# Layer 2 attention: scores of a pair of heads in one block, value products in one block, output projection in one burst

## The chip, the core and the metric

The kernel runs on one core of one Trainium2 chip. The metric is the device time of one execution in microseconds (us). A core has five engines with their own in-order instruction streams, which meet only through semaphores: TensorE (PE; its weight loads are listed as PEld), VectorE (DVE), ScalarE (ACT), GpSimd (POOL) and SyncE (SP). Matmuls write to PSUM, which has eight banks of 128 partitions x 512 float32.

## The reference

Four layers run one after the other over 16 sequences of 256 tokens and 128 channels (4096 tokens). Each layer computes `x = x + attention(layernorm(x)) * silu(ffn(layernorm(x)))`. The change touches the attention of layer 2 alone:

```python
q = z @ wq @ fcq_w + fcq_b          # 16 heads of 64 channels; k and v likewise
scores = jnp.einsum('bihd,bjhd->bhij', q, k) / scale
attn = jax.nn.softmax(scores, axis=-1)
out = jnp.einsum('bhij,bjhd->bihd', attn, v)
return out.reshape(b, n, 16 * 64) @ fco_w + fco_b
```

The feed-forward part of layer 2 is a mixture of eight experts (two chosen for each token). The kernel runs it in the same loop as the attention.

## The kernel before

**Tiling.** Tokens are taken in eight groups of 512 (two sequences each, called batch elements 0 and 1 of the group). Sixteen heads make eight pairs. A pair of heads of one group is a "pair"; there are 64. A pair and one batch element is a "unit" `n`; there are 128 (`ALL`). A unit has two halves, one for each head: half `h = 2n + half`. All matmuls are float32, and the trace shows each as two instructions.

**The loop.** `Layer2.tensor`, `.scalar` and `.vector` walk over the same slots, one unit for each slot, and each engine does, in this written order, what is due at a lag behind the slot (`due(slot, lag)`):

- PE: scores of unit `slot` (`tensor_score`, both halves, 64 rows of the array for each); in some slots a value projection ("v", called V below); transposes of half 0 of unit `slot - 2` (`tensor_turn`, T0 below); the product with the values of unit `slot - 3` (`tensor_times_v`, 64 columns of the array for each head); the projection of the next pair's q or k ("qk"); transposes of half 1 of unit `slot - 2` (T1); every second slot the output projection of a finished pair (`tensor_fold`); then expert work (`tensor_experts`: in even slots down and place, in odd slots up, from slot 32 to 104).
- DVE: reciprocal of the sums and normalisation of half 0 of unit `slot - 1`; the two row maxima of unit `slot` (`vector_max`); the V eviction; the copy of T0's bank to `pt` (`vector_turned`, unit `slot - 2`); normalisation of half 1 of unit `slot - 1`; the q or k eviction; routing or notes (`vector_notes`, even slots).
- ACT: expert evictions of the slot before; four exponentials of unit `slot` (`scalar_exp`); the copy of T1's bank (`scalar_turned`); every second slot the copy of the value products (`scalar_outputs`).
- POOL normalises the first 12 units, then issues indirect DMAs.

V occurs in slots 4 to 7 and 12 to 15 of every 16, that is in half of the pairs. The 64 pairs thus split in pairs with V and pairs without. I call slots 32 to 104, with expert work in each, the heavy slots, and the slots without expert matmuls the light ones. Slots 108 to 111 and 118 to 121 hold the joins of expert results, which keep PE busy far longer than a light slot.

**Waits and banks.** There is one bank for the transposes (`b_turn`): T1 of a unit waits for DVE's copy of T0, and T0 of the next unit waits for ACT's copy of T1 (`wait_turned_scores`). Scores have three banks; V and q/k projections share `b_misc`, and each waits until the last result there has been evicted. The scores of a pair wait for its q and k evictions (`l2_qk`). The output projection has a bank of its own (`b_fo`) in which it accumulates over eight slots' worth of pairs.

Of the kernel before, what the change touches and what calls it, by code (L numbers as in the profile page):

```python
# [12 lines left out]
P = 128  # L13
BATCH, SEQ = 16, 256
TOKENS = BATCH * SEQ
GW = 512
# [1828 lines left out]
L2_UNITS = BPG * L2_PAIRS  # L1845


class Layer2:
# [5 lines left out]
    def __init__(self, k, n, nth):  # L1854
# [12 lines left out]
        self.p, self.pt, self.o, self.mixed = work.ring(6), work.ring(4), region.ring(2), work.ring(GROUPS)  # L1867
# [3 lines left out]
        self.b_score, self.b_moe, self.b_turn, self.b_o, self.b_misc, self.b_fo = b[0:3], b[3], b[4], b[5], b[6], b[7]  # L1871
# [74 lines left out]
    def shared_bank(self, slot, kind):  # L1946

        return (self.b_misc, self.b_fo)[self.shared_count(slot, kind) % 2 if slot < 0 else 0]
# [21 lines left out]
    def vector_shared(self, v, on, slot, kinds):  # L1970
        s = self.k.sem
        for kind, g, i in self.shared(slot):
            if kind not in kinds:
                continue
            if kind == "v":
                c, t = divmod(i, TPG)
                on.wait_ge(s["l2_misc"], self.shared_count(slot, "v"))
                on.wait_ge(s["l2_pv"], L2_UNITS * (g - 1) + L2_UNITS // 2 * (c + 1))
# [15 lines left out]
    def tensor_score(self, pe, on, n, half):  # L1994
# [4 lines left out]
        on.wait_ge(s["l2_exp"], 2 * (h - 2))  # L1999
        q, kk = self.q[pair % 2][r, t], self.kk[pair % 2][r, t]  # L2000
        for i in range(2):
            last = mm(pe, self.b_score[h % 3][:, i * SEQ:(i + 1) * SEQ], q[:, i * P:(i + 1) * P], kk)
        last.then_inc(s["l2_score"], 1)

    def vector_max(self, v, on, n, half):
# [3 lines left out]
        v.tensor_reduce(self.mx[h % 8][:, 0:2], self.b_score[h % 3][:, :].rearrange("p (i j) -> p i j", j=SEQ), AX.X,  # L2009
# [6 lines left out]
    def scalar_exp(self, a, on, n, half):  # L2016
# [4 lines left out]
        for i in range(2):  # L2021
            c = slice(i * SEQ, (i + 1) * SEQ)
            a.activation(self.p[h % 6][:, c], self.b_score[h % 3][:, c], ACT.Exp, bias=self.mx[h % 8][:, i:i + 1],  # L2023
# [33 lines left out]
    def vector_turned(self, v, on, n):  # L2057
        s, h = self.k.sem, 2 * n
        on.wait_ge(s["l2_pt_mm"], h + 1)
        on.wait_ge(s["l2_pv"], n - 1)  # L2060
        v.tensor_copy(self.pt[h % 4], self.b_turn[:, :]).then_inc(s["l2_pt"], 1)  # L2061

    def scalar_turned(self, a, on, n):
        s, h = self.k.sem, 2 * n + 1
        on.wait_ge(s["l2_pt_mm"], h + 1)
        on.wait_ge(s["l2_pv"], n - 1)
        a.activation(self.pt[h % 4], self.b_turn[:, :], ACT.Copy).then_inc(s["l2_pt_act"], 1)

    def tensor_times_v(self, pe, on, n):
        s = self.k.sem  # L2070
        g, m, b = self.unit(n)
        self.wait_turned_scores(on, 2 * n)
        self.wait_turned_scores(on, 2 * n + 1)
        on.wait_ge(s["l2_v"], 8 * g + 4 * (m // 4) + 4)
        on.wait_ge(s["l2_o"], n // BPG)
        for jc in range(2):
            for half in range(2):
                h, r = 2 * m + half, half * L2_DH
                c = slice((h % 8) * L2_DH, (h % 8 + 1) * L2_DH)
                last = mm(pe, self.b_o[r:r + L2_DH, b * SEQ:(b + 1) * SEQ], self.v[2 * b + jc][h // 8][:, c],  # L2080
                          self.pt[(2 * n + half) % 4][:, jc * SEQ:(jc + 1) * SEQ], first=jc == 0, last=jc == 1)
        last.then_inc(s["l2_pv"], 1)

    def scalar_outputs(self, a, on, pair):
        s = self.k.sem
        on.wait_ge(s["l2_pv"], 2 * pair + 2)
        on.wait_ge(s["l2_fold"], pair - 1)
        a.activation(self.o[pair % 2], self.b_o[:, :], ACT.Copy).then_inc(s["l2_o"], 1)

    def tensor_fold(self, pe, on, pair):  # L2090
        s = self.k.sem
        g, m = divmod(pair, L2_PAIRS)
        on.wait_ge(s["l2_o"], pair + 1)
        if m == 0:
            on.wait_ge(s["l2_mixed"], g)
        mm(pe, self.b_fo[:, :], self.Fo[:, m, :], self.o[pair % 2], first=m == 0, last=m == L2_PAIRS - 1).then_inc(s["l2_fold"], 1)

    def scalar_mixed(self, a, on, g):
        s = self.k.sem
        on.wait_ge(s["l2_fold"], L2_PAIRS * (g + 1))  # L2100
        a.activation(self.mixed[g], self.b_fo[:, :], ACT.Identity, bias=self.o_b).then_inc(s["l2_mixed"], 1)
# [90 lines left out]
    def pair_end(self, slot, lag):  # L2192
        n = slot - lag
        return n // BPG if 0 <= n < self.ALL and n % BPG == BPG - 1 else None

    def tensor(self, pe, on):
# [5 lines left out]
        for slot in range(self.FIRST, self.LAST):  # L2202
# [10 lines left out]
            if (n := self.due(slot, 3)) is not None:  # L2213
                self.tensor_times_v(pe, on, n)
# [3 lines left out]
            if (n := self.pair_end(slot, 4)) is not None:  # L2218
                self.tensor_fold(pe, on, n)
            self.tensor_experts(pe, on, slot)  # L2220

    def scalar(self, a, on):
# [4 lines left out]
        for slot in range(self.FIRST, self.LAST):  # L2227
# [9 lines left out]
            if (n := self.pair_end(slot, 3)) is not None:  # L2237
                self.scalar_outputs(a, on, n)
            if (n := self.pair_end(slot, 4)) is not None and n % L2_PAIRS == L2_PAIRS - 1:
                self.scalar_mixed(a, on, n // L2_PAIRS)  # L2240
# [1635 lines left out]
```

## Time and profile before

| | us |
|---|---|
| median of 3 runs (range) | 2921.56 (2917.99 to 2922.57) |
| span of the profiled execution | 2983.9 |
| layer 2's loop in that span, from its first scores to its last output | 1357 to 2170 |
| slots 32 to 104 of it | 1566 to 2001 |

The span runs from the first to the last instruction of the profiled execution; no time outside of the span is recorded for it. The span is 62.3 us over the median of the timed runs. Over the whole span PE is busy 90%, DVE 65%, ACT 44% and POOL 42%.

### The profile page before, as it was taken

To read this page: it belongs to the slowest core of one execution; us is meant where nothing else is said; L and a number is where in the kernel's file an instruction comes from. 1 tells how busy PE (TensorE), PEld (TensorE's weight loads), DVE (VectorE), ACT (ScalarE), POOL (GpSimd) and SP (SyncE) were. 2 spreads that over 40 slices of the span, in tenths; PEclk is the share of its full clock that TensorE was granted. 3 is DMA by queue.
4 is the path that set the end of the run, shared out by engine and by line. 5 is a ranking of instruction groups with operands and counts; after the bars stand their busy time and mean duration, and the time that the engine had idled before them with its cause. 6 is when DMAs were issued, how large, how long until landed. Compare 5 with 4: busy or idle time off the path is not lost.

```text
span 2983.9 us, 40531 instructions
## 1 busy us (share of the span) xinstructions
PE 2684.1 (90%) x14378; PEld 1731.9 (58%) x14378; DVE 1941.2 (65%) x3806; ACT 1320.6 (44%) x3421; POOL 1239.8 (42%) x1116
## 2 busy tenths in 40 slices
PE   6899699999999999978879999999987988988888
PEld 3465245555555555544446666665546877766766
DVE  5778576877877777647657777776665272646633
ACT  4454424334344344344446666664542223355442
POOL 2553067677677677734542333320001340333331
PEclk8899799999999999989999999999977776889898
DMA  4453200000000000028012222211002211212113
GB/s 164 137 181 113 98 1 1 1 1 1 1 1 1 1 1 1 1 92 214 31 49 56 65 69 67 69 52 41 8 32 94 68 57 43 60 29 65 33 47 92
DMA packets 172520, 159.55 MB, mean 53 GB/s; under 512 B 98736, under 2 KB 149168, under 8 KB 171504
## 3 DMA queue, kind: packets, MB, share of 16 engines
q1 hardware_dynamic: 149536, 90.92, 10.9%
q0 software_dynamic: 22784, 66.05, 7.2%
q8 instruction: 115, 1.88, 0.3%
q14 instruction: 85, 0.70, 0.1%
HBM read 127.16 MB, written 59.51 MB: 63 GB/s over the span
## 4 chain that ended last, share of the span: by engine, by line
PE 42%; DVE 7%; ACT 3%; issue 2%; another core or an unknown queue 1%; DMA 0%; POOL 0%; SPq 0%; POOLq 0%; DVEq 0%; ACTq 0%
PE bank L65 37%; PE bank L2053 4%; DVE work L2009 1%; DVE work L3289 1%; ACT L3231 1%; DVE work L3071 0%; ACT weights_odd L2937 0%; DVE work L3337 0%; DVE work L1986 0%; DVE weights_odd L3339 0%; DVE weights_odd L3337 0%; DVE work L3488 0%; PE bank L2884 0%; DVE weights_even L3289 0%
## 5 line engine op out<-in xcount | busy, mean ns | idle before, releaser
L1492 POOL TENSOR_TENSOR work<-work 128x512 f32<-128x512 f32 x384 | 494.8, 1289 | 305.6 <-DVE work L1484 285.4
L65 PE MATMUL bank<-work 64*128 64x256 f32 (+5 forms) x4384 | 588.2, 351 | 23.4 <-DVE work L3488 7.2
L65 PE MATMUL bank<-weights_odd,normed_channels 128*128 128x512 f32 (+3 forms) x1152 | 520.4, 561 | 52.7 <-DVE work L1484 52.0
L65 PEld LDWEIGHTS bank<-work 64*128 64x128 f32 (+4 forms) x4384 | 412.4, 171 | 225.1 <-issue 144.7
L1484 DVE TENSOR_TENSOR work<-bank,work 128x512 f32<-128x512 f32 x360 | 244.4, 685 | 104.2 <-PE bank L65 100.3
L2023 ACT ACTIVATE work<-bank,work 128x256 f32<-128x256 f32 x512 | 236.0, 472 | 156.3 <-DVE work L2009 145.9
L65 PEld LDWEIGHTS bank<-weights_odd,normed_channels 128*128 128x128 f32 x1152 | 187.4, 198 | 183.2 <-DVE work L1484 94.2
L2009 DVE TENSOR_REDUCE work<-bank 128x2 f32<-128x512 f32 x256 | 165.3, 685 | 172.3 <-PE bank L65 151.5
L595 POOL DMA_INDIRECT weights_even<-in_L_Wx,expert_slots x112 | 111.6, 996 | 355.6 <-PE bank L668 270.9
L1559 ACT ACTIVATE work<-bank,work 128x256 f32<-128x256 f32 x256 | 119.0, 470 | 290.1 <-DVE work L1546 289.9
L65 PE MATMUL bank<-work,weights_odd 128*128 128x512 f32 (+3 forms) x520 | 209.3, 518 | 34.3 <-ACT work L3253 9.0
L65 PE MATMUL bank<-weights_even,work 128*128 128x128 f32 (+4 forms) x1568 | 219.4, 300 | 14.8 <-ACT work L3037 7.0
L65 PEld LDWEIGHTS bank<-weights_even,work 128*128 128x128 f32 (+2 forms) x1568 | 202.3, 206 | 30.9 <-issue 14.4
L2053 PEld LDWEIGHTS bank<-constants,work 128*128 128x128 f32 x1024 | 122.9, 142 | 149.0 <-issue 131.2
L65 PE MATMUL bank<-work,weights_even 32*128 32x128 f32 (+4 forms) x800 | 170.7, 403 | 39.9 <-DVE work L1037 11.4
L2053 PE MATMUL bank<-constants,work 128*128 128x128 f32 x1024 | 160.6, 280 | 21.9 <-DVE work L2061 10.3
L65 PE MATMUL bank<-weights_even 128*128 128x128 f32 (+3 forms) x940 | 175.5, 342 | 5.3 <-ACT work L3267 2.1
L2919 POOL TENSOR_TENSOR weights_odd<-weights_odd 128x512 f32<-128x512 f32 x40 | 52.4, 1309 | 291.1 <-ACT weights_odd L2914 291.1
L65 PE MATMUL bank<-weights_odd 128*128 128x128 f32 (+3 forms) x664 | 146.9, 373 | 8.2 <-ACT weights_odd L2891 5.9
L585 POOL DMA_INDIRECT noted_rows<-work,expert_slots x96 | 99.1, 1032 | 114.9 <-DVE work L575 88.4
L2041 DVE TENSOR_SCALAR work<-work 128x256 f32<-128x256 f32 x464 | 143.8, 352 | 4.1
L1621 POOL TENSOR_TENSOR work<-work 128x512 f32<-128x512 f32 x120 | 135.7, 1141 | 18.8 <-DVE work L1611 12.9
(343 smaller groups left out, 4633.6 us busy)
## 6 DMA issues: line engine op xcount, KB each, us to landing
filter_matrices<-in_L_filters SPq DMA_DIRECT2D x24, 512.0 KB, 8.1
work<-filter_matrices SPq DMA_DIRECT2D x16, 768.0 KB
weights_even<-noted_rows SPq DMA_DIRECT2D x56, 132.0 KB
noted_rows<-in_empty SPq DMA_DIRECT2D x11, 660.0 KB, 10.3
noted_rows_in<-in_empty SPq DMA_DIRECT2D x8, 660.0 KB, 10.2
weights_odd<-noted_rows_in SPq DMA_DIRECT2D x40, 132.0 KB
work<-token_rows SPq DMA_DIRECT2D x16, 256.0 KB, 3.0
token_rows_out<-in_zeros SPq DMA_DIRECT2D x6, 640.0 KB, 20.1
```

The source lines that it names most:

```text
L65: return pe.matmul(out, lhsT, rhs, start=first, stop=last, skip_group_check=True)
L585: gp.indirect_dma_start(self.x_rows[:, :], to, self.stage[g % len(self.stage)][:, i, :], None).then_inc(k.sem[f"rows_moved{self.moved_by(g ...
L595: gp.indirect_dma_start(self.W_of(m, i), None, self.weights, of).then_inc(self.k.sem[f"weights_moved{m % self.ring}"], 16)
L1484: v.tensor_tensor(heads(dst), heads(self.b_prod[p % 2][:, :]), self.per_head(self.score[g % 3], tile, kind == 0, e), ALU.mult).then_inc(s[ ...
L1492: gp.tensor_tensor(self.sum_of(p), self.sum_of(p), self.product_of(p), ALU.add).then_inc(s["l1_add"], 1)
L1559: a.activation(self.p[n % 2][:, c], self.b_score[n % 2][:, c], ACT.Exp, bias=self.mx[n % 4][:, i:i + 1], accum_out=self.sums(bt)[:, h, i:i ...
L1621: gp.tensor_tensor(self.kept[n % 2].rearrange("p (d h) -> p h d", h=L1_H), heads(self.o[i]), self.per_head(self.mask[g % 3], tile, 1, e), ...
L2009: v.tensor_reduce(self.mx[h % 8][:, 0:2], self.b_score[h % 3][:, :].rearrange("p (i j) -> p i j", j=SEQ), AX.X, ALU.max, negate=True).then ...
L2023: a.activation(self.p[h % 6][:, c], self.b_score[h % 3][:, c], ACT.Exp, bias=self.mx[h % 8][:, i:i + 1], accum_out=self.sums(n, half, i)). ...
L2041: eng.tensor_scalar(p[:, c], p[:, c], self.sums(n, half, i), None, ALU.mult).then_inc(s["l2_p"], 1)
L2053: last = pe.transpose(self.b_turn[:, jc * SEQ + i * P:jc * SEQ + (i + 1) * P], self.p[h % 6][:, i * SEQ + jc * P:i * SEQ + (jc + 1) * P], ...
L2919: gp.tensor_tensor(h, h, self.factor[n % 2], ALU.mult).then_inc(self.k.sem["moe_scaled"], 1)
```

## The change

In even slots PE now computes the scores of both batch elements of a pair (sixteen score instructions instead of eight, into four banks), then the value products of both batch elements of an older pair (lag 4 slots). Odd slots have neither. T0, q/k, T1 and the expert work stay one unit for each slot. The output projection is no longer done pair by pair: all eight pairs' value products are kept (`self.o`, eight buffers of region 1), and one burst of eight matmuls runs at slot 3 of the next group, in `b_misc`; `b_fo` becomes the fourth score bank. DVE's and ACT's written orders stay as they are, but for the waits' constants and the place of `scalar_outputs` and `scalar_mixed`.

```diff
-        self.b_score, self.b_moe, self.b_turn, self.b_o, self.b_misc, self.b_fo = b[0:3], b[3], b[4], b[5], b[6], b[7]
+        self.b_score, self.b_moe, self.b_turn, self.b_o, self.b_misc = [*b[0:3], b[7]], b[3], b[4], b[5], b[6]
+        self.b_ahead = b[7]
...
-        on.wait_ge(s["l2_exp"], 2 * (h - 2))
+        on.wait_ge(s["l2_exp"], 2 * (h - 3))
+        if h == 3:
+            on.wait_ge(*self.shared_free[1])
...
-    def tensor_times_v(self, pe, on, n):
+    def tensor_times_v(self, pe, on, pair):
...
+        for b in range(BPG):
+            n = BPG * pair + b
+            self.wait_turned_scores(on, 2 * n)
+            self.wait_turned_scores(on, 2 * n + 1)
...
+    def tensor_fold(self, pe, on, g):
+
+        s = self.k.sem
+        on.wait_ge(s["l2_o"], L2_PAIRS * (g + 1))
+        on.wait_ge(*self.shared_free[0])
+        self.shared_free[0] = (s["l2_mixed"], g + 1)
+        for m in range(L2_PAIRS):
+            last = mm(pe, self.b_misc[:, :], self.Fo[:, m, :], self.o[m], first=m == 0, last=m == L2_PAIRS - 1)
+        last.then_inc(s["l2_fold"], 1)
...
+    def fold_due(self, slot):
+        return event(slot, L2_UNITS + 3, L2_UNITS, 0, GROUPS)
...
-            if (n := self.due(slot, 0)) is not None:
-                self.tensor_score(pe, on, n, 0)
-                self.tensor_score(pe, on, n, 1)
+            if (pair := self.pair_due(slot, 0)) is not None:
+                for n in range(BPG * pair, BPG * (pair + 1)):
+                    self.tensor_score(pe, on, n, 0)
+                    self.tensor_score(pe, on, n, 1)
+            if (pair := self.pair_due(slot, 4)) is not None:
+                self.tensor_times_v(pe, on, pair)
             self.tensor_shared(pe, on, slot, ("v",))
             if (n := self.due(slot, 2)) is not None:
                 self.tensor_turn(pe, on, n, 0)
-            if (n := self.due(slot, 3)) is not None:
-                self.tensor_times_v(pe, on, n)
             self.tensor_shared(pe, on, slot, ("qk",))
             if (n := self.due(slot, 2)) is not None:
                 self.tensor_turn(pe, on, n, 1)
-            if (n := self.pair_end(slot, 4)) is not None:
-                self.tensor_fold(pe, on, n)
+            if (g := self.fold_due(slot)) is not None:
+                self.tensor_fold(pe, on, g)
             self.tensor_experts(pe, on, slot)
```

PE before, one even and one odd heavy slot without V: scores are `128x256 x4`, value products `64x256 x4`, transposes L2053, the q/k projection reads `normed_channels`, the single `weights_even 128x512` is the output projection, and the rows behind T1 are expert work.

```order
L65 MATMUL bank<-work 128x256 x4
L2053 MATMUL bank<-constants,work 128x128 x4
L65 MATMUL bank<-work 64x256 x4
L65 MATMUL bank<-normed_channels,weights_even 128x512
L2053 MATMUL bank<-constants,work 128x128 x4
L65 MATMUL bank<-weights_even,work 128x128 x4
L668 MATMUL bank<-constants,weights_even 128x128 x2
L65 MATMUL bank<-work 128x256 x4
L2053 MATMUL bank<-constants,work 128x128 x4
L65 MATMUL bank<-work 64x256 x4
L65 MATMUL bank<-normed_channels,work 128x512
L2053 MATMUL bank<-constants,work 128x128 x4
```

PE in the changed kernel, the same kind of two slots (transposes are now L2058):

```order
L65 MATMUL bank<-work 128x256 x8
L65 MATMUL bank<-work 64x256 x8
L2058 MATMUL bank<-constants,work 128x128 x4
L65 MATMUL bank<-normed_channels,weights_even 128x512
L2058 MATMUL bank<-constants,work 128x128 x4
L65 MATMUL bank<-weights_even,work 128x128 x4
L668 MATMUL bank<-constants,weights_even 128x128 x2
L2058 MATMUL bank<-constants,work 128x128 x4
L65 MATMUL bank<-normed_channels,work 128x512
L2058 MATMUL bank<-constants,work 128x128 x4
L65 MATMUL bank<-weights_even 128x128 x4
```

The odd slot has lost its scores and value products; both now stand ahead of the even slot's T0. DVE in the changed kernel, from the copy of T0 in an even slot (L2066) to the copy of T0 in the odd slot; L2046 is the normalisation, L1989 the q/k eviction, L627 to L632 the notes, L2034 the reciprocal, L2014 the row maxima:

```order
L2066 COPY work<-bank 128x512
L2046 TENSOR_SCALAR work<-work 128x256 x2
L1989 TENSOR_SCALAR work<-bank,weights_even 128x512
L627 TENSOR_TENSOR work<-weights_even,work 128x2
L629 SCALAR_TENSOR_TENSOR expert_slots<-work,weights_even 128x2
L630 TENSOR_TENSOR work<-work,weights_even 128x2
L632 TENSOR_TENSOR work<-work,weights_even 128x2
L2034 RECIPROCAL work<-work 128x4
L2046 TENSOR_SCALAR work<-work 128x256 x2
L2014 TENSOR_REDUCE work<-bank 128x2 x2
L2066 COPY work<-bank 128x512
```

Nothing moved here: this is also the order before, but for line numbers.

## Rows read from the trace of the kernel before

**Rows 1.** Windows: length; PE, PEld, DVE, ACT, POOL busy; PEclk; DMA share; GB/s.

```profile
1357.00:1424.00 67.00, 58.67 (x307) 31.25 (x307) 54.53 (x129) 31.31 (x111) 41.17 (x45) 0.99 0.80 180
1424.00:1566.00 142.00, 115.87 (x592) 61.91 (x590) 85.59 (x197) 61.32 (x199) 69.12 (x72) 0.93 0.13 42
1566.00:2001.00 435.00, 435.00 (x2659) 273.87 (x2659) 317.73 (x830) 275.21 (x937) 136.97 (x138) 1.00 0.23 63
2001.00:2170.00 169.00, 162.63 (x906) 95.86 (x906) 106.61 (x240) 84.28 (x259) 1.91 (x2) 0.98 0.09 26
```

**Rows 2.** Timeline: start, duration, engine. PE scores opening slots 48 and 64.

```profile
1662.17 1.14 PE L65 MATMUL bank<-work 64*128 64x256 f32 x8
...
1758.94 1.14 PE L65 MATMUL bank<-work 64*128 64x256 f32 x8
```

**Rows 3.** Timeline of slot 42 (even, heavy), with the openings of slots 43 and 44.

```profile
1624.97 1.14 PE L65 MATMUL bank<-work 64*128 64x256 f32 x8
...
1626.04 0.66 PE L2053 MATMUL bank<-constants,work 128*128 128x128 f32 x4
1626.13 1.29 DVE L2009 TENSOR_REDUCE work<-bank 128x2 f32<-128x512 f32 x2 [1.72 <-PE bank L65]
...
1626.62 1.08 PE L65 MATMUL bank<-work 128*64 128x256 f32 x8
...
1627.64 1.13 PE L65 MATMUL bank<-normed_channels,weights_even 128*128 128x512 f32 x2
...
1628.60 0.60 PE L2053 MATMUL bank<-constants,work 128*128 128x128 f32 x4
...
1628.80 0.75 DVE L1986 TENSOR_SCALAR work<-bank,weights_even 128x512 f32<-128x512 f32 x1 [0.26 <-PE bank L65]
...
1629.04 1.06 PE L65 MATMUL bank<-weights_even,work 128*128 128x128 f32 x8
...
1629.47 0.15 DVE L627 TENSOR_TENSOR work<-weights_even,work 128x2 f32<-128x2 f32 x1
...
1630.00 0.17 DVE L2029 RECIPROCAL work<-work 128x4 f32<-128x4 f32 x1
1630.21 0.61 DVE L2041 TENSOR_SCALAR work<-work 128x256 f32<-128x256 f32 x2
...
1630.24 1.14 PE L65 MATMUL bank<-work 64*128 64x256 f32 x8
...
1636.16 1.14 PE L65 MATMUL bank<-work 64*128 64x256 f32 x8
```

**Rows 4.** Narrow timeline cuts of PE in slot 42: second and last score pair, second q/k.

```profile
1625.29 0.39 PE L65 MATMUL bank<-work 64*128 64x256 f32 x2
...
1625.72 0.39 PE L65 MATMUL bank<-work 64*128 64x256 f32 x2
...
1628.17 0.59 PE L65 MATMUL bank<-normed_channels,weights_even 128*128 128x512 f32 x1
```

**Rows 5.** Timeline: from the q/k eviction to the waiting scores (slot 4).

```profile
1373.95 0.75 DVE L1986 TENSOR_SCALAR work<-bank,weights_even 128x512 f32<-128x512 f32 x1 [0.79 <-PE bank L65]
...
1374.76 0.49 PE L65 MATMUL bank<-work 64*128 64x256 f32 x2 [0.41 <-DVE work L1986]
```

**Rows 6.** Timeline: from DVE's copy to normalisation, and to the waiting T1.

```profile
2152.47 0.68 DVE L2061 COPY work<-bank 128x512 f32<-128x512 f32 x1
...
2153.06 0.60 DVE L2041 TENSOR_SCALAR work<-work 128x256 f32<-128x256 f32 x2
...
2153.29 0.63 PE L2053 MATMUL bank<-constants,work 128*128 128x128 f32 x4 [0.46 <-DVE work L2061]
```

**Rows 7.** Timeline: from T0 to DVE's waiting copy.

```profile
2158.45 0.63 PE L2053 MATMUL bank<-constants,work 128*128 128x128 f32 x4
...
2159.12 0.69 DVE L2061 COPY work<-bank 128x512 f32<-128x512 f32 x1 [0.58 <-PE bank L2053]
```

**Rows 8.** Windows, columns as in rows 1: a stretch with a stall of PE.

```profile
1440.00:1450.00 10.00, 7.82 (x34) 3.81 (x33) 6.29 (x15) 3.73 (x11) 4.85 (x5) 0.83 0.10 34
```

More of the change, by code:

```diff
@@ L1866, in __init__ @@
         self.q, self.kk = work.ring(2), work.ring(2)
[L1867 removed]
+        self.p, self.pt, self.mixed = work.ring(6), work.ring(4), work.ring(GROUPS)
+        self.o = Arena(k.regions[1], L2_OUTPUTS[1], L2_OUTPUTS[0]).ring(L2_PAIRS)
         self.mx, self.rs = work.ring(8, 8), work.ring(4, 8)
@@ L1946, in shared_bank @@
     def shared_bank(self, slot, kind):
-        return (self.b_misc, self.b_fo)[self.shared_count(slot, kind) % 2 if slot < 0 else 0]
+        return (self.b_misc, self.b_ahead)[self.shared_count(slot, kind) % 2 if slot < 0 else 0]
     def wait_shared(self, on, slot, kind, sem, n):
@@ L2065, in scalar_turned @@
         on.wait_ge(s["l2_pt_mm"], h + 1)
-        on.wait_ge(s["l2_pv"], n - 1)
+        on.wait_ge(s["l2_pv"], n // BPG)
         a.activation(self.pt[h % 4], self.b_turn[:, :], ACT.Copy).then_inc(s["l2_pt_act"], 1)
-    def tensor_times_v(self, pe, on, n):
+    def tensor_times_v(self, pe, on, pair):
         s = self.k.sem
-        g, m, b = self.unit(n)
-        self.wait_turned_scores(on, 2 * n)
-        self.wait_turned_scores(on, 2 * n + 1)
+        g, m = divmod(pair, L2_PAIRS)
         on.wait_ge(s["l2_v"], 8 * g + 4 * (m // 4) + 4)
[L2075 to L2081, printed above, removed]
+        on.wait_ge(s["l2_o"], pair)
+        for b in range(BPG):
+            n = BPG * pair + b
+            self.wait_turned_scores(on, 2 * n)
+            self.wait_turned_scores(on, 2 * n + 1)
+            for jc in range(2):
+                for half in range(2):
+                    h, r = 2 * m + half, half * L2_DH
+                    c = slice((h % 8) * L2_DH, (h % 8 + 1) * L2_DH)
+                    last = mm(pe, self.b_o[r:r + L2_DH, b * SEQ:(b + 1) * SEQ], self.v[2 * b + jc][h // 8][:, c],
+                              self.pt[(2 * n + half) % 4][:, jc * SEQ:(jc + 1) * SEQ], first=jc == 0, last=jc == 1)
         last.then_inc(s["l2_pv"], 1)
@@ L2085, in scalar_outputs @@
         s = self.k.sem
[L2086 to L2090, printed above, removed]
+        on.wait_ge(s["l2_pv"], pair + 1)
+        on.wait_ge(s["l2_fold"], pair // L2_PAIRS)
+        a.activation(self.o[pair % L2_PAIRS], self.b_o[:, :], ACT.Copy).then_inc(s["l2_o"], 1)
+    def tensor_fold(self, pe, on, g):
         s = self.k.sem
[L2092 to L2096, printed above, removed]
+        on.wait_ge(s["l2_o"], L2_PAIRS * (g + 1))
[4 more added lines that the diff above has]
+        last.then_inc(s["l2_fold"], 1)
     def scalar_mixed(self, a, on, g):
         s = self.k.sem
-        on.wait_ge(s["l2_fold"], L2_PAIRS * (g + 1))
-        a.activation(self.mixed[g], self.b_fo[:, :], ACT.Identity, bias=self.o_b).then_inc(s["l2_mixed"], 1)
+        on.wait_ge(s["l2_fold"], g + 1)
+        a.activation(self.mixed[g], self.b_misc[:, :], ACT.Identity, bias=self.o_b).then_inc(s["l2_mixed"], 1)
     def vector_route(self, v, on):
@@ L2190, in due, with pair_due @@
         return slot - lag if 0 <= slot - lag < self.ALL else None
-    def pair_end(self, slot, lag):
+    def pair_due(self, slot, lag):
         n = slot - lag
-        return n // BPG if 0 <= n < self.ALL and n % BPG == BPG - 1 else None
+        return n // BPG if 0 <= n < self.ALL and n % BPG == 0 else None
+    def fold_due(self, slot):
+        return event(slot, L2_UNITS + 3, L2_UNITS, 0, GROUPS)
     def tensor(self, pe, on):
@@ L2236, in scalar @@
                 self.scalar_turned(a, on, n)
[L2237 to L2240, printed above, removed]
+            if (pair := self.pair_due(slot, 4)) is not None:
+                self.scalar_outputs(a, on, pair)
+            if (g := self.fold_due(slot)) is not None:
+                self.scalar_mixed(a, on, g)
     def vector(self, v, on):
```

11 lines of the change are left out of this document (6 added, 5 removed).

## The prediction

> **What bounds the kernel now.** I read the windows over layer 2 first [rows 1]. From 1566 to 2001 us, slots 32 to 104, PE is busy for 435 of 435 us at a granted clock of 1.00, DVE for 318, ACT for 275. PE is the bound there, and no other engine decides. From 2001 to 2170 PE is busy 163 of 169 us. From 1424 to 1566 it is busy 116 of 142 us at 0.93, and from 1357 to 1424 59 of 67. Slots 48 to 64, one group of eight pairs, take 1758.94 - 1662.17 = 96.8 us [rows 2]. Then I read one slot on the timeline [rows 3]: the reader is to see that between T0 and T1 there are value products and a q/k projection (1626.62 to 1628.60), and between T1 and the next T0 the expert work and scores. DVE's copy of T0's bank and ACT's copy of T1's bank lie beside these, and PE never waits for them. DVE is slowed by nothing and idles 1.72 us before the maxima.
>
> **The gain in PE's own work.** A block of scores takes 1.07 us from its start to T0's [rows 3], but inside of it a pair of score instructions costs (1625.72 - 1625.29) / 2 = 0.215 us [rows 4], so four pairs are 0.86. The rest, 0.21, is spent on changing the array's layout from full to two row halves and back. Value products take 1.02, again 0.16 over 0.86. T0, between two layouts, takes 0.58; T1, with full-array work on both sides, 0.44. The first q/k instruction costs 0.53 behind value products, the second 0.43 [rows 3, 4]. A slot thus loses 0.21 + 0.16 + 0.14 + 0.10 = 0.61, and with the entry of scores behind expert work (0.09) 0.70 us, 1.40 for a pair of slots. The changed pair has full to rows, rows to columns, columns to full: some 0.5 is left. So PE's own work falls by 0.9 us for each pair, 64 pairs: 58 us. The page "TensorEngine Tiling (Array Packing)" of the Trainium skill, section Key Properties, says that a change of tiling mode drains TensorE. The trace agrees (0.14 to 0.21 for a block), and by that rule alone the change makes the kernel faster; it is the first rival below.
>
> **What the regrouping uncovers.** I lay out the changed pair from the start of its score block (time 0), heavy slots, no V, with these parts: scores 1.07 + 0.86 = 1.93; value products 1.02 + 0.86 = 1.88; so T0 starts at 3.81. In between DVE has only a normalisation and the two maxima of the even unit, done by about 2.4, and it is in order: the next thing is its copy of T0's bank. It idles until T0 is done.
> - T0 start to DVE's copy: 0.67 [rows 7].
> - Copy to normalisation 0.59 [rows 6]; a normalisation pair lasts 0.61 and the next starts some 0.07 before its end: 0.54.
> - q/k eviction to the notes 0.67, notes 0.53, reciprocal 0.21 [rows 3], normalisation of the even unit 0.54, two maxima of the odd unit 1.29 - 0.07 = 1.22.
> - DVE's copy of the odd unit's T0, to T1 on PE: 0.82 [rows 6].
>
> The sum is 0.67 + 0.59 + 0.54 + 0.67 + 0.53 + 0.21 + 0.54 + 1.22 + 0.82 = 5.79. The odd unit's T1 cannot start before 3.81 + 5.79 = 9.60. PE's own way there is T0 0.50, q/k 0.86, a 0.13 wait, T1 0.44, down and place 1.64 - 0.53 = 1.11, T0 0.44, q/k 0.86: it arrives at 8.15 and waits 1.45. Behind T1: 0.44, the ups 0.90 (slot 43 is 5.92 long, slot 42 5.27: 5.92 - 5.27 + 1.11 - 0.86 for the output projection), 0.09 into the next scores. The pair takes 11.03. Before it took 11.19 with its output projection [rows 3], 10.33 without. So the loop scores, products, T0, DVE chain, T1, experts, scores has a length of its own, 0.70 us longer than PE's old work. What used to cover DVE (scores between T1 and T0, products between T0 and T1) has moved in front of the chain.
>
> ACT is not in this loop: the odd unit's exponentials start 0.73 behind its first maximum and end by some 10.1, before the next scores. I cost the fourth score bank at nothing for that reason; without it the scores would wait.
>
> **With V** (half of the pairs) V and q/k share a bank, and the value products no longer lie between them. A V start to its DVE eviction takes about 1.1 (q/k's is 1.16 [rows 3]), and 0.82 back. By the same steps: T0 at 4.67; q/k at 5.7; its eviction at 6.8; notes, reciprocal, normalisation and maxima to 9.96; V eviction; q/k of the odd slot at 10.8, T1 at 11.64, next scores at 13.06. Before: 10.33 + 4 x 0.43 = 12.1 [rows 4]. The pair loses 0.9. (Old group by these parts: 4 x 10.33 + 4 x 12.1 + 8 x 0.86 = 96.6, where the rows have 96.8 [rows 2].)
>
> **The output projection.** Sixteen instructions of 0.43 either way; the burst is full-array work, no layout change more. It waits for the odd slot's q/k eviction (same bank), which in the layout above lies 0.7 behind T1: 0.7 for each group. The last burst stands alone at the end: seven projections of 0.86 that lay inside the loop before now follow the last value products, but no work is added to the sum; against the old tail it is 6 us later. At the lower clock it would be up to 12; I take 6.5.
>
> **Light slots** lack notes and experts. The chain is 5.26, T1 at 9.07, but the next scores wait for the odd q/k eviction: copy at 8.25, + 0.59 + 0.54 + 0.81 [rows 5] = 10.19. Before: 10.33 - 1.11 - 0.90 = 8.3. They lose 1.9 a pair, with V 12.2 against 10.1, 2.1.
>
> **Sum**, against the span of 2983.9:
> - slots 32 to 103, 4.5 groups of 4 x 0.70 + 4 x 0.9 + 0.7 = 7.1: +32
> - slots 104 to 127: seven light pairs +13, pair 104 +1, four join pairs, whose long PE work hides DVE, -1: +13
> - end: +6.5
> - slots 12 to 31, ten pairs: by the chain 4 x 1.9 + 6 x 2.1 = +20. But they took 142 us, where PE's work is 102, so 40 us are stalls and half-clock stretches that I can't attribute; if these lie beside the new waits it is 0. I take +14.
> - slots 0 to 11: POOL normalises, DVE has routing work in its place; 0 to +8, I take +4.
>
> Together +69. The timed runs are 62 us under the span; the stalls may well be shorter in them, but the chain's terms are durations that both share. 2921.56 + 69 = 2991; I forecast 2988 us. Own range, from the unknown terms: 2965 to 3015.
>
> **Rivals.**
> 1. PE stays the bound. Then 58 is gained and 6 lost at the end: 2870. For it: 435 of 435 us busy, and the DVE share of 73% looks like room. Against: the room is in the wrong place; DVE is in order, and its odd-slot maxima stand ahead of the copy that T1 needs. It would need the chain to be 1.5 us shorter than I count.
> 2. Heavy slots come out even (the chain 0.7 shorter, through steps that overlap more than I assumed), only light ones lose: 2955.
> 3. PE's idle time costs clock. At 1440 to 1450 us PE is busy 7.8 of 10 and the granted clock is 0.83 [rows 8]; a stretch at 1.2 GHz doubles PE's parts. In the changed light pairs PE is busy 7.4 of 10.2. If a third of 18 light pairs ran at half clock, + 6 x 7.4 = 44: 3035. The page "TensorE: Matmul & The Clock Gate" of the Trainium skill, in its section on oscillation, has the same rule: idle gaps bring the lower rate back. Against: heavy pairs are busy 9.4 of 11.0 with gaps of 1.5, and stretches of slots 0 to 11 with 59 of 67 were granted 0.99 [rows 1].
>
> **Chances.** My forecast 0.70, rival 1 0.08, rival 2 0.12, rival 3 0.10. The range 2945 to 3020 takes in the forecast's and rival 2's. Faster by over 0.2% (what a measurement of this kernel tells from no change) 0.08, within 0.02, slower 0.90.
>
> **What would show it.** In the new profile: PE busy in the heavy stretch falls from 100% to some 86%, with waits of about 1.4 us of T1 (L2058) on DVE's copy (L2066), one for each pair; DVE idle of 1.5 to 2 us before the copy of the even slot; a heavy group of some 104 us in place of 96.8; score blocks of sixteen instructions of 1.93 us; eight light pairs at 10 to 12. I am wrong if T1 doesn't wait, or if PE waits elsewhere for longer, such as for ACT or for the shared bank.

## The result, and the profile after

The changed kernel takes 3010.93 us (median of 4 runs, 3008.71 to 3015.19) against 2922.07 us for the kernel before (4 runs, 2917.99 to 2927.93). The ratio on record for these runs is 1.0291, with an interval of 1.0273 to 1.0309 (the two medians alone divide to 1.0304). It is slower by 89 us where 66 were forecast (2988 against 2921.56), inside the range of 2945 to 3020.

The two profiled spans differ by only 3012.8 - 2983.9 = 28.9 us. The span shown of before held some 37 us of stalls in slots 12 to 31 (142.6 us against 105.8) that a profile of the same code but for one blank (c0_before, span 2920.9) doesn't have. In the first profile DVE and ACT wait there for something that the trace doesn't record. Rows of waits over 1420 to 1570 (engine and line, what it waited for, total us, times, longest):

```profile
DVE work L2009 <- remote: 20.6, 12, 2.8
ACT work L2067 <- remote: 12.5, 4, 3.5
DVE work L2061 <- remote: 4.5, 4, 1.5
```

`remote` stands for an event that the trace doesn't hold. Over the same stretch c0_before has no such row. I therefore compare with c0_before. Windows of the changed kernel, slots 0 to 11, 12 to 31, 32 to 103, and 104 to the first matmul of layer 3; then ten us of a burst that is read below. The columns are those of [rows 1].

```profile
1354.60:1425.50 70.90, 55.22 (x286) 33.45 (x286) 52.49 (x125) 30.89 (x110) 39.52 (x44) 0.90 0.74 166
1425.50:1548.00 122.50, 103.58 (x589) 60.85 (x588) 83.45 (x196) 60.05 (x200) 70.43 (x73) 1.00 0.15 48
1548.00:2028.50 480.50, 429.58 (x2666) 283.24 (x2666) 314.03 (x832) 275.40 (x936) 140.06 (x138) 0.99 0.21 57
2028.50:2215.80 187.30, 161.10 (x920) 100.20 (x919) 107.81 (x243) 85.70 (x261) 2.08 (x3) 0.98 0.08 24
1674.00:1684.00 10.00, 9.40 (x22) 4.28 (x23) 1.77 (x6) 1.26 (x5) 2.10 (x2) 0.83 0.18 59
```

The same windows of c0_before:

```profile
1360.70:1423.80 63.10, 55.89 (x302) 30.35 (x302) 51.72 (x125) 31.13 (x110) 41.17 (x45) 1.00 0.82 182
1423.80:1529.60 105.80, 105.80 (x594) 58.90 (x593) 85.86 (x198) 60.87 (x199) 69.66 (x72) 1.00 0.18 56
1529.60:1964.20 434.60, 434.60 (x2657) 273.78 (x2656) 317.77 (x830) 275.06 (x935) 137.31 (x138) 1.00 0.23 63
1964.20:2133.90 169.70, 161.05 (x907) 95.49 (x906) 108.03 (x242) 86.25 (x261) 1.92 (x2) 0.99 0.09 26
```

Layer 2 takes 861.2 us instead of 773.2, so 88.0 of the 91.9 us between these spans lie in it. In slots 32 to 103 PE was busy for the whole 434.6; now it is busy 429.6 of 480.5. PE's work has fallen and the stretch has grown: the new time is waiting. One heavy pair without V, PE and DVE (start, duration, engine, line; line numbers of the changed kernel: T0 and T1 L2058, DVE's copy L2066, normalisation L2046, q/k eviction L1989, maxima L2014):

```profile
1604.46 3.98 PE L65 MATMUL bank<-work 64*128 64x256 f32 x32
...
1606.49 1.49 PEld L65 LDWEIGHTS bank<-work 128*64 128x64 f32 x16 [0.33 <-issue]
...
1608.38 0.66 PE L2058 MATMUL bank<-constants,work 128*128 128x128 f32 x4
...
1609.07 0.69 DVE L2066 COPY work<-bank 128x512 f32<-128x512 f32 x1 [2.15 <-PE bank L2058]
...
1610.20 0.74 DVE L1989 TENSOR_SCALAR work<-bank,weights_even 128x512 f32<-128x512 f32 x1
...
1611.39 0.17 DVE L2034 RECIPROCAL work<-work 128x4 f32<-128x4 f32 x1
1611.48 0.60 PE L2058 MATMUL bank<-constants,work 128*128 128x128 f32 x4
...
1612.12 1.28 DVE L2014 TENSOR_REDUCE work<-bank 128x2 f32<-128x512 f32 x2
...
1613.32 0.68 DVE L2066 COPY work<-bank 128x512 f32<-128x512 f32 x1
...
1614.15 0.63 PE L2058 MATMUL bank<-constants,work 128*128 128x128 f32 x4 [1.21 <-DVE work L2066]
...
1615.60 0.49 PE L65 MATMUL bank<-work 64*128 64x256 f32 x2
```

This is the loop of the prediction. Scores and products run as one stretch (the products' weight loads begin at 1606.49); DVE idles 2.15 us until T0 is there; then no idle time of DVE is recorded from 1609.07 to the second copy; PE waits 1.21 us for that copy; then come the ups and the next scores. From T0 to the odd unit's T1 it is 1614.15 - 1608.38 = 5.77 us, where 5.79 was summed. The pair takes 11.14 (11.03 forecast, 10.33 before without its projection).

The rows of waits for slots 32 to 103 of the changed kernel, all that PE's matmuls waited for by over 1 us in sum:

```profile
PE bank L65 <- DVE work L1982: 25.3, 36, 1.1
PE bank L2058 <- DVE work L2066: 21.9, 18, 1.3
PE bank L65 <- DVE work L1989: 3.2, 6, 0.6
```

The 18 pairs without V wait for DVE's copy (21.9 / 18 = 1.22 each). The 18 pairs with V wait twice each for DVE to evict V (L1982), since q/k then needs the same bank. The wait is 0.35 in the even slot, which is the bank's own round trip, and 1.06 in the odd slot, where DVE evicts V behind the maxima and is late, as laid out in the prediction. The burst's rows, in slot 51 and at the end of the layer:

```profile
1674.04 0.63 PE L2058 MATMUL bank<-constants,work 128*128 128x128 f32 x4 [1.21 <-DVE work L2066]
1675.22 8.80 PE L65 MATMUL bank<-weights_odd,weights_even 128*128 128x512 f32 x16 [0.56 <-DVE work L1989]
1683.86 0.83 PE L65 MATMUL bank<-weights_even 128*128 128x128 f32 x6
...
2203.71 1.95 PE L65 MATMUL bank<-work 128*64 128x256 f32 x16
2206.36 7.13 PE L65 MATMUL bank<-weights_odd,weights_even 128*128 128x512 f32 x16 [0.70 <-ACT weights_odd L2096]
2215.79 1.55 PE L65 MATMUL bank<-x_channels,constants 128*128 128x512 f32 x3 [2.30 <-DVE x_channels L821]
```

The burst waits 0.56 us for the q/k eviction. In this group it then lasts 8.6 us where sixteen instructions of 0.43 are 6.9: the window above has a granted clock of 0.83 there, so about a third of its ten us was at the lower of the two levels, 1.2 GHz, and the rest at 2.4.

### The profile page after: what moved, and what is told of

The parts are those of the page before. It is cut to its first block, busy times and chain, and to the rows that moved or that the text cites. A ratio compares the mean times of both kernels' runs of the same rounds, so it can differ in the third digit from the quotient of the medians.

```text
span 3012.8 us, 40357 instructions
## 1 busy us (share of the span) xinstructions
PE 2648.3 (88%) x14378; PEld 1735.6 (58%) x14378; DVE 1933.6 (64%) x3806; ACT 1319.0 (44%) x3421; POOL 1243.2 (41%) x1116
## 4 chain that ended last, share of the span: by engine, by line
PE 37%; DVE 14%; ACT 3%; issue 2%; DMA 0%; POOL 0%; SPq 0%; DVEq 0%; ACTq 0%
PE bank L65 34%; DVE work L2014 2%; DVE work L2046 2%; PE bank L2058 2%; DVE work L1989 1%; DVE work L1982 1%; DVE work L2066 1%; ACT L3245 1%; DVE work L3303 1%; ACT weights_odd L2951 0%; DVE weights_even L3303 0%; DVE work L3085 0%; DVE weights_odd L3353 0%; DVE weights_odd L3351 0%; PE bank L2898 0%
## 5 line engine op out<-in xcount | busy, mean ns | idle before, releaser
L65 PE MATMUL bank<-work 64*128 64x256 f32 (+5 forms) x4384 | 556.9, 349 | 22.7 <-DVE work L3502 7.2
L65 PEld LDWEIGHTS bank<-work 64*128 64x128 f32 (+4 forms) x4384 | 430.9, 171 | 213.7 <-issue 129.6
L2028 ACT ACTIVATE work<-bank,work 128x256 f32<-128x256 f32 x512 | 235.8, 473 | 106.2 <-DVE work L2014 105.8
L2014 DVE TENSOR_REDUCE work<-bank 128x2 f32<-128x512 f32 x256 | 164.1, 683 | 114.3 <-PE bank L65 114.3
L2058 PEld LDWEIGHTS bank<-constants,work 128*128 128x128 f32 x1024 | 118.9, 141 | 185.2 <-issue 157.3
L2058 PE MATMUL bank<-constants,work 128*128 128x128 f32 x1024 | 159.7, 279 | 52.6 <-DVE work L2066 34.5
L2072 ACT ACTIVATE work<-bank 128x512 f32<-128x512 f32 x128 | 76.4, 597 | 208.5 <-PE bank L2058 207.3
L2046 DVE TENSOR_SCALAR work<-work 128x256 f32<-128x256 f32 x464 | 142.9, 350 | 4.1
L1621 POOL TENSOR_TENSOR work<-work 128x512 f32<-128x512 f32 x120 | 135.8, 1142 | 20.9 <-DVE work L1611 12.9
L644 POOL DMA_INDIRECT token_rows<-weights_even,expert_slots x112 | 115.7, 1033 | 64.2 <-issue 32.6
```

Of the source, the lines that this page charges most:

```text
L65: return pe.matmul(out, lhsT, rhs, start=first, stop=last, skip_group_check=True)
L644: gp.indirect_dma_start(self.y_rows[:, :], to, self.place_y[m % 2][:, i * P:(i + 1) * P], None).then_inc(self.k.sem[f"rows_moved{2 + m % 2 ...
L1621: gp.tensor_tensor(self.kept[n % 2].rearrange("p (d h) -> p h d", h=L1_H), heads(self.o[i]), self.per_head(self.mask[g % 3], tile, 1, e), ...
L2014: v.tensor_reduce(self.mx[h % 8][:, 0:2], self.b_score[h % 4][:, :].rearrange("p (i j) -> p i j", j=SEQ), AX.X, ALU.max, negate=True).then ...
L2028: a.activation(self.p[h % 6][:, c], self.b_score[h % 4][:, c], ACT.Exp, bias=self.mx[h % 8][:, i:i + 1], accum_out=self.sums(n, half, i)). ...
L2046: eng.tensor_scalar(p[:, c], p[:, c], self.sums(n, half, i), None, ALU.mult).then_inc(s["l2_p"], 1)
```

## The experiments

My theory: PE's loop now holds a chain of DVE work that PE's work no longer covers. The rivals: PE pays for the regrouping itself (layout, clock); the burst costs the time; DVE is simply too full. All times below are us; a pair is given without V / with V, heavy slots, without the output projection.

| kernel | median | ratio to before [95%] | heavy pair |
|---|---|---|---|
| c0_before | 2925.09 | 1.002 [1.0006, 1.0034] | 10.33 / 12.14 |
| e1_max_early | 2953.40 | 1.0111 [1.0091, 1.0131] | 9.94 / 12.52 |
| e6_extra_chain | 3055.04 | 1.0454 [1.0429, 1.048] | 11.74 / 13.84 |
| e7_extra_gap | 3020.45 | 1.0333 [1.0309, 1.0356] | 11.14 / 13.24 |
| e2_scores_only | 3001.46 | 1.0042 [1.0013, 1.0071] | 10.21 / 11.95 |
| e3_products_only | 3043.55 | 1.0198 [1.0143, 1.0253] | 10.80 / 12.95 |
| e4_burst_only | 3009.64 | 1.0058 [1.0026, 1.009] | 10.33 / 12.14 |
| e8_split | 3007.80 | 1.0067 [1.0035, 1.0098] | 10.24 / 12.16 |
| c1_after | 3071.72 | 1.0291 [1.0265, 1.0316] | 11.14 / 13.24 |
| e9_products_ahead | 3012.50 | 1.0094 [1.0072, 1.0116] | 10.35 / 12.98 |
| e10_experts_between | 3014.76 | 1.0093 [1.0071, 1.0115] | 10.12 / 13.15 |
| e11_heavy_order | 3011.62 | 1.0052 [1.003, 1.0073] | 10.49 / 12.98 |

The first four ran on one chip (before: 2919.8), the next four on a second (2994.9), three on a third (2986.9), the last on a fourth (2992.4). Only ratios are compared across chips.

**c0_before** is the kernel before with one blank added, to see how far two builds agree.

> The kernel before, once more, for a second trace. The first trace has a span of 2983.9 us, 62 over the timed median, and 40 us of stalls in slots 12 to 31 of layer 2 that the changed kernel's trace doesn't have. If the stalls belong to that one execution: span about 2922 to 2930, slots 12 to 31 in some 102 us, and two traces then differ by the same 89 us as the times. If they belong to the old order: about 142 us there again.

It measured 1.002, at the edge of what I call no change. Its profile has 105.8 us in slots 12 to 31 where the first had 142.

**e1_max_early** puts all four maxima of a pair on DVE behind the even unit's score block, so that they fall in DVE's idle 2.15 us and leave the chain:

```diff
-            if (n := self.due(slot, 0)) is not None:
-                self.vector_max(v, on, n, 0)
-                self.vector_max(v, on, n, 1)
+            if (pair := self.pair_due(slot, 0)) is not None:
+                for n in range(BPG * pair, BPG * (pair + 1)):
+                    self.vector_max(v, on, n, 0)
+                    self.vector_max(v, on, n, 1)
```

> The changed kernel, with the row maxima of both units of a pair taken in the even slot, where DVE is idle before T0's copy. Chain theory: 1.22 us leave the chain of every pair from T0's copy to the odd unit's T1. Heavy pairs without V from 11.14 to 9.9, with V from 13.24 to 12.0, light ones from 10.25 to 9.35; in all 60 to 70 us less than the changed kernel: about 2945. Rival, that PE's new block order itself costs the time (bank hand-overs, layout changes between row and column halves, a lower clock): no PE instruction moves, so 3011 within 5.

A pair without V fell from 11.14 to 9.94, by 1.20: the maxima's 1.22 in the sum, and just the 1.21 of the wait. A pair with V fell only from 13.24 to 12.52. All that PE's matmuls waited for by over 1 us in sum, 1600 to 2000:

```profile
PE bank L65 <- DVE work L1982: 11.1, 32, 0.3
...
PE bank L65 <- DVE work L1989: 2.7, 5, 0.6
```

The wait for the copy (L2066) is gone, and of the wait for V's eviction 0.35 per slot stays, which is the shared bank's own round trip. The same DVE work, in another place, gave back 1.8 of 2.9 per cent (1.0111 for 1.0291), or 53 of 85 us. "DVE too full" falls with that, and so does "PE pays for the regrouping itself": PE's instructions stand as in the changed kernel, and a pair without V takes 9.94, less than the 10.33 before. Pairs with V missed the 12.0 expected. What e1 still loses against c0_before is 9.6 us in slots 12 to 31, 8.1 in slots 32 to 103 (where the two kinds of pair cancel and the five bursts and four moved projections stay) and 8.7 at the end.

**e6_extra_chain and e7_extra_gap** add one DVE addition that nobody needs to each pair (it lasts 0.68 us, and the next instruction starts 0.60 behind it), e6 behind the odd unit's maxima, inside the chain, and e7 behind the even unit's, in the gap (`== 0` in place of `== 1`; the buffer's own line is left out here):

```diff
+                if n % BPG == 1 and n >= self.BY_GPSIMD:
+                    v.tensor_tensor(self.spare, self.Fk[:, 0:GW], self.Fk[:, GW:2 * GW], ALU.add)
```

> The changed kernel with one more DVE instruction (a sum of two 128x512 tiles that nobody reads, about 0.65 us) behind the odd unit's maxima, in the chain, from unit 12 on (58 pairs). Chain theory: 0.6 x 50 or so, the join pairs absorb it: +30 to +38, 3041 to 3049. Rival (PE's own order or DVE's share of busy time is no bound): 3011 within 5.

> The same added instruction as in the run before, but behind the even unit's maxima, in DVE's idle time ahead of T0's copy. Chain theory: 3011 within 5, as DVE has over 1.5 us there (with V a little less). A theory by which DVE's total work is the bound: the same +30 to +38 as when it stands in the odd slot.

In the chain each pair grew by 0.60 (11.74 / 13.84), all of it as wait. The same rows of waits of e6, 1600 to 2000 (its lines are one higher):

```profile
PE bank L65 <- DVE work L1983: 30.2, 30, 1.7
PE bank L2059 <- DVE work L2067: 25.4, 14, 1.8
```

25.4 / 14 = 1.81, against 1.22. The whole time grew by 44 us (3055 against 3011), more than the 30 to 38 expected: 58 x 0.6 is 35, and by the profile some 6 of the rest lie at the end. In the gap the pairs stayed at 11.14 / 13.24. But e7's ratio is still 0.4% above the changed kernel's, where the theory has nothing. Its profile has 868.3 us for layer 2 against 861.2: nothing in slots 32 to 103, -3.1 in slots 0 to 11, +3.6 in slots 104 to 125 (in one burst pair and one join pair) and +6.8 behind them, at the layer's end. The end is not the added instruction's doing: c1_after below, the changed kernel but for a blank, has 33.8 us there where the changed kernel has 28.0 and e7 34.8. In both of the long ones the last value products run at the lower clock (3.68 us in place of 1.95; granted 0.77 over 22 us around them, where the changed kernel has 1.00). In the loop itself the gap is free.

**e4_burst_only, e2_scores_only, e3_products_only** take the change apart. All keep the burst. e4 has scores and products unit by unit as before, e2 has the score block, e3 the product block. The waits' constants and ACT's copy of the value products follow these orders and are left out here. e3's edit on the changed kernel:

```diff
-            if (pair := self.pair_due(slot, 0)) is not None:
-                for n in range(BPG * pair, BPG * (pair + 1)):
-                    self.tensor_score(pe, on, n, 0)
-                    self.tensor_score(pe, on, n, 1)
+            if (n := self.due(slot, 0)) is not None:
+                self.tensor_score(pe, on, n, 0)
+                self.tensor_score(pe, on, n, 1)
```

and e2's (e4 is both):

```diff
-            if (pair := self.pair_due(slot, 4)) is not None:
-                self.tensor_times_v(pe, on, pair)
...
                 self.tensor_turn(pe, on, n, 0)
+            if (n := self.due(slot, 3)) is not None:
+                self.tensor_times_v(pe, on, n)
```

> Scores and value products unit by unit as in the kernel before; only the burst of the output projection and the fourth score bank stay. Each burst waits about 0.5 for the q/k eviction, and the last one, alone at the end, costs 6: 2926 to 2934. If the burst is worse than I think (clock, the shared bank), 2940 or over; if it costs nothing, 2920.

> The changed kernel with the value products back at their old place, unit by unit between T0 and q/k (lag 3); the score block of sixteen and the burst stay. Chain theory: both copies are covered again in heavy slots, PE is the bound and a heavy pair without V takes 10.0 (10.33 before without its output projection); in light slots the odd T0 waits 0.9 for ACT's copy, as the odd slot's scores no longer lie there: 8.9 against 8.33. In all 2925 to 2935, near the kernel before. Rival (the score block itself costs the time): near 3000.

> The changed kernel with the scores back unit by unit at the head of every slot; the block of value products and the burst stay. Chain theory: the odd slot's scores again separate T1 from the next T0, but the products no longer separate T0 from T1: heavy pairs without V 10.7, light ones 9.4: 2960 to 2975. Rival (grouped products are harmless and all of the loss comes from the score block and its late maxima): at or under 2935.

The burst alone leaves the pairs at 10.33 / 12.14 and costs 17.87 - 10.33 - 6.88 = 0.66 in its own pair, and some 6 us in the tail (26.5 against 20.6). The score block saves 0.12 / 0.19 a pair. The product block costs 0.47 / 0.81. Together they would cost 0.35 / 0.62; the changed kernel costs 0.81 / 1.10. So some 0.47 a pair is neither block's own, but comes from having both. PE's waits in e3 over 1600 to 2000:

```profile
PE bank L65 <- DVE work L1982: 13.1, 32, 0.5
PE bank L2058 <- DVE work L2066: 9.1, 15, 0.6
```

The wait for the copy is 0.6 there and 1.22 with both blocks. One block takes away one of two covers: products between T0 and T1, or scores between T1 and T0. With the products left (e2) DVE keeps up, and PE has no wait for it in that stretch; with the scores left (e3) it nearly does. e2's heavy pairs (10.0 expected) and light ones (9.52, 8.9 expected) came out longer than I had laid out.

**e8_split** keeps the score block, puts the maxima early as e1, and moves one unit's products ahead of T0 in every slot (lag 4), so that T0 to T1 has q/k alone beside DVE's copy (the burst goes behind the expert work). Its main edit, on top of e2's order:

```diff
+            if (n := self.due(slot, 4)) is not None:
+                self.tensor_times_v(pe, on, n)
             if (n := self.due(slot, 2)) is not None:
                 self.tensor_turn(pe, on, n, 0)
-            if (n := self.due(slot, 3)) is not None:
-                self.tensor_times_v(pe, on, n)
```

> A version after the chain theory: scores in one block, the maxima of both units in the even slot, value products unit by unit ahead of T0 in every slot (lag 4; they cover ACT's copy of T1 and the V eviction), the burst behind the expert work. Five layout changes a pair in place of eight (three in the changed kernel). Heavy pairs without V 9.8 (10.33 before), with V 11.6 (12.14), light ones as before; tail +6: 2900 to 2912. Rival (layout changes or clock rule): between before and the changed kernel, as it has its order of changes in between.

A miss: 10.24 / 12.16 instead of 9.8 / 11.6. One even slot of e8, PE:

```profile
1777.20 0.66 PE L2058 MATMUL bank<-constants,work 128*128 128x128 f32 x4
1777.69 1.02 PE L65 MATMUL bank<-normed_channels,weights_even 128*128 128x512 f32 x2
1778.73 0.63 PE L2058 MATMUL bank<-constants,work 128*128 128x128 f32 x4
```

T1 comes 1.53 behind T0. That is T0 to DVE's copy 0.7 and copy to T1 0.82, the round trip of the one transpose bank; T0 and q/k fill 0.49 + 0.86 = 1.35 of it. The rest, 0.17 to 0.18, is lost twice a pair where q/k alone stands between T0 and T1, also in e1 (1.53 in the even slot for 1.35 of work, 1.48 in the odd slot for 1.30).

**c1_after** is the changed kernel with a blank, beside before on a third chip.

> The changed kernel once more, on the chip of this set, so that the runs here are compared with both. Ratio to the kernel before 1.027 to 1.031 as in the first comparison; if this chip is one on which slots 12 to 31 stall for 40 us in every kernel, 1.020 to 1.031.

The ratio is 1.0291 again, though both kernels are 2% slower there. Slots 12 to 31 take 153.9 us in it against 122.6 in the first profile, while slots 32 to 103 take 480.5 and 480.4.

**e9_products_ahead, e10_experts_between, e11_heavy_order** look for a better order, starting from the kernel before: e9 moves products ahead of T0 (and V), e10 also puts expert work between q/k and T1, e11 does both only in heavy slots and keeps V ahead of the products. e11:

```diff
+            if heavy:
+                self.tensor_times_v(pe, on, slot - 3)
             if (n := self.due(slot, 2)) is not None:
                 self.tensor_turn(pe, on, n, 0)
-            if (n := self.due(slot, 3)) is not None:
+            if (n := self.due(slot, 3)) is not None and not heavy:
                 self.tensor_times_v(pe, on, n)
             self.tensor_shared(pe, on, slot, ("qk",))
+            if heavy:
+                self.tensor_experts(pe, on, slot)
             if (n := self.due(slot, 2)) is not None:
                 self.tensor_turn(pe, on, n, 1)
...
-            self.tensor_experts(pe, on, slot)
+            if not heavy:
+                self.tensor_experts(pe, on, slot)
```

> The kernel before, with the value products ahead of V and T0 in every slot (lag 4 in place of 3) and nothing in blocks: scores, products, T0, q/k, T1. Three layout changes a slot in place of four, which saves about 0.2, but T0 and T1 are now only q/k apart (0.86, where DVE's copy takes 1.49 from T0 to T1): each slot waits 0.13 to 0.18 there. Chain theory: 0.99 to 1.00 of before, heavy pairs without V 10.2 to 10.4 (their output projection not counted). Layout rule alone: 0.4 a pair, 0.991.

> As the run before, with the expert work between q/k and T1, where it covers DVE's copy; ACT's copy of T1 is covered by the next slot's scores and products. Heavy pairs lose the layout change and no wait comes: 0.3 to 0.4 a pair less than before, 36 pairs, 11 to 15 us; light slots as in the run before. 0.994 to 0.997 of before. If PE's own work isn't shortened by one layout change less a slot: 1.000 or over.

> The kernel before, but in slots 33 to 103 PE goes scores, V, value products (lag 3 as before), T0, q/k, expert work, T1, output projection; the other slots keep the old order. V's eviction is covered by the products, T0's copy by q/k and experts, T1's copy by the next scores. One layout change less in a slot without V, none less with V. Chain theory: pairs without V 10.98 in place of 11.19 (with their projection), pairs with V 12.8 to 13.0 in place of 14.01 in the run before, which had V next to T0: heavy stretch 426 to 431 in place of 434.6, ratio to the kernel before 0.997 to 0.999. Rival (V pairs were slow there for another reason than their bank): V pairs near 14, ratio over 1.004.

All three are slower than before, and all three expectations of the time missed. Without V, e10 gains 0.21 a pair, e9 nothing, and e11 loses 0.16 (in all but one of these pairs PE waits 0.2 for ACT's copy of the value products). With V, e9 and e10 lose 0.84 and 1.01. V and q/k follow each other in one bank there, with T0 alone between them, and PE waits 0.35 in each of the two slots, 0.70 of the loss; the rest is not taken apart. From e9:

```profile
1793.22 1.12 PE L65 MATMUL bank<-weights_even,normed_channels 128*128 128x512 f32 x2
1794.18 0.60 PE L2053 MATMUL bank<-constants,work 128*128 128x128 f32 x4
1795.13 1.12 PE L65 MATMUL bank<-normed_channels,weights_even 128*128 128x512 f32 x2 [0.35 <-DVE work L1979]
```

e11 was to avoid that, and a wait of another kind took its place, in 15 of the 18 heavy pairs with V:

```profile
1799.66 0.66 PE L2053 MATMUL bank<-constants,work 128*128 128x128 f32 x4
...
1801.99 0.69 DVE L2061 COPY work<-bank 128x512 f32<-128x512 f32 x1 [2.42 <-remote]
...
1802.83 0.63 PE L2053 MATMUL bank<-constants,work 128*128 128x128 f32 x4 [0.75 <-DVE work L2061]
```

The copy starts 2.33 us behind T0's start, where 0.67 is usual [rows 7]. Nothing in the trace ended that wait at 1801.99, and I can't say what did. The three other pairs with V (slots 46, 84 and 102) have no such wait and take 12.91 with their projection. That is inside the 12.8 to 13.0 expected, 0.93 under the others and 0.09 under the 13.00 before. So the order does for V's bank what it was made for, and the unexplained wait is what pairs with V lose in e11. No kernel here beats the one before.

## Why the prediction was right, and where its sizes were off

**The mechanism** held step by step: T0 to T1 5.77 (5.79 summed), DVE idle 2.15 before the even copy, T1 waiting once a pair. e6 and e7 show that DVE's place in the loop sets the time and not its load, e1 that the odd maxima are the length of the wait.

| term | forecast | measured against c0_before |
|---|---|---|
| slots 0 to 11 | +4 | +7.8 |
| slots 12 to 31 | +14 | +16.8 |
| slots 32 to 103 | +32 | +45.8 |
| slots 104 to 127 (measured: to 125) | +13 | +10.1 |
| end (measured: from 126) | +6.5 | +7.5 |
| sum | +69 | +88 (and +4 outside layer 2) |

**Heavy slots, 14 us short.** Three parts.

- Pairs: 0.81 instead of 0.70, and 1.10 instead of 0.9; 18 x 0.11 + 18 x 0.20 = 5.6. In both kinds 0.10 of it is the score block: it takes 2.03 (1604.46 to 1606.49, where the products begin), not 1.07 + 0.86 = 1.93. I applied the step "inside of it a pair of score instructions costs 0.215" [rows 4] to a block twice as long. It holds there but for one place: from the fifth pair of instructions to the sixth, in every such block of the trace, the second instruction comes 0.31 behind its forerunner (1605.45 to 1605.76), and what follows is 0.10 late. No run tells why. The other 0.1 with V is a rounding of mine: the layout gave 13.06 against 10.33 + 4 x 0.43 = 12.05, a loss of 1.0, and I entered 0.9.
- I counted 4.5 groups of projections, but five bursts fall in slots 32 to 103, in place of 36 projections spread over them: 4 x 0.86 = 3.4, moved from elsewhere and not lost.
- Two of the five bursts ran in part at the lower clock, 1.7 us each (20.50 against 18.80 for the pair), 3.4 in all; and the wait was 0.80 for 0.70 per burst.

Together 5.6 + 3.4 + 3.4 + 0.5 = 12.9 of 13.8.

**PE's own gain** was over-estimated at 0.9 a pair. Without the wait the pair would take 11.14 - 1.20 = 9.94, which is what e1 measures. That is 0.39 under 10.33. The rest: the score block saves 0.1 less; T0 to T1 with q/k alone between them is bound by the round trip of the one transpose bank (1.53 in e8), which takes 0.17 twice; the last 0.07 is hundredths in several steps. In the same way PE was busy 89% of slots 32 to 103 (429.6 of 480.5), where 86% were forecast. So rival 1 (PE stays the bound, 2870) was wrong in its own price as well: at 0.39 for 64 pairs, less 6 at the end, it would have been about 2903. The page "TensorEngine Tiling (Array Packing)" of the Trainium skill, section Key Properties, says that a change of tiling mode drains TensorE. e2 against e4 takes away one block's entry and exit a pair and gains 0.12. That agrees with the rule, and it is a tenth of the 1.21 that T1 waits in the changed kernel.

**Early and light slots.** Light pairs took 10.25 (10.19 forecast) and 12.29 with V (12.2). Slots 104 to 125 lost 2.9 less than forecast: eleven projections of 0.86 left them and one burst of 6.9 came in, 2.6 less, which my sum left out as it did in the heavy slots. That it comes out so closely is partly luck: the pair of slot 112 took 13.5 us in c0_before, with waits and a granted clock of 0.87, and 11.3 in the changed kernel, and the last light pair is counted in the end. Slots 0 to 11 lost 3.8 more, within the 0 to 8 that I gave; their granted clock was 0.90 where c0_before has 1.00, and I did not test what brought it down.

**The stalls of slots 12 to 31**, which I could not attribute, are not part of the order. They are in the first profile of before and in every profile from the second to the fourth chip, and not in those from the first chip or in the first profile of the changed kernel. They are 37 of the 63 us by which the first profile of before is longer than c0_before; 25 more lie behind layer 2 (811.6 us against 787.0) and are not taken apart. So the two first profiles differed by 28.9 us where the timed runs differed by 89.

**Rival 2** (heavy slots even) fell with 11.14. **Rival 3** (clock) was half right and in another place. The light pairs that I priced ran at a granted 1.00, though PE was busy only 103.6 of 122.5 us. The drop came in bursts: 0.83 over 1674 to 1684, where PE was busy 9.4 of 10. Before it PE had idled 1.21 and 0.56 us within 2 us.

The page "TensorE: Matmul & The Clock Gate" of the Trainium skill, section HAM oscillation, says that a wait between groups of matmuls brings the lower rate back; its example waits for DMA. The trace agrees only in part: three of the five bursts in slots 32 to 103 lie behind the same two waits and ran at 1.00, and the pairs without a burst, with the same wait of 1.21, had a granted 1.00 (1590 to 1660 us). Over all runs, 9 of the 20 bursts of heavy slots ran in part at the lower clock (8.5 to 8.8 us in place of 7.1) in the four profiles in which PE waited 1.2 to 1.8 us for the copy just before them (changed kernel, c1_after, e6, e7). None of the 25 did in e1, e2, e3, e4 and e8, where that wait was 0.61 or none. In the bursts it is worth some 5 of the 88 us.

## What to carry to other kernels

Before you group work of the engine that is the bound, ask for each piece what it covers on the next engine: here PE's own work fell by 0.39 us a pair and a wait of 1.20 us came in, since both pieces that lay beside an in-order evictor's chain were moved in front of it. Write out the loop (producer, chain, consumer, back to the producer) and compare its length with the bound's work; shares of busy time (here 73% for DVE) do not show it. If such a loop is too long, move work out of the chain into the evictor's gap (1.20 us of 1.21 regained in e1), and check which bank two neighbours now share.

## What the runs showed that I had not expected

- Two blocks cost more than their sum: +0.81 a pair against -0.12 and +0.47.
- A block of sixteen row-half score instructions takes 2.03 us and one of eight 1.07 with the same switch behind it, so merging two saves 0.11, not the 0.21 that the first block's surplus over 0.215 a pair suggests. Half of that surplus comes back as one late step inside the longer block.
- Code that differs by a blank ran at 2919.8 to 2925 us on one chip and the kernel before at 2987 to 2995 on three others. In every profile from the three others slots 12 to 31 hold some 30 to 45 us more, and in those whose waits I read (c1_after, e3, e4, e9, and the first profile of before) DVE and ACT have 23 to 39 us of waits there that no recorded event ends. The ratio stayed the same (1.0291 twice).
- In e11 DVE's copy starts 1.7 us late in 15 of 18 heavy pairs with V, and no recorded event ends the wait. Its cause stays open.
